# New step orders for the heads of attentions 2 to 4, two masked groups on GpSimd instead of three, and one home for the query operand

## The reference

```python
x = x + _L0_xattn_ref(_layernorm(x), ctx, ctx, fside, mask, ...)   # softmax(QK + mask) * group_prob
x = x + _L1_xattn_ref(_layernorm(x), ctx, ctx, mask, ...)          # where(m == 0, -1e9, scores)
x = x + _L2_xattn_ref(ctx, ctx, _layernorm(x), mask_b, ...)        # one row of key mask
x = x + _L3_xattn_ref(_layernorm(x), ctx, ctx, ...)                # no mask
```

## Time and profile before

| | us |
|---|---|
| runs, timed: median (lowest to highest) | 1549.96 (1547.44 to 1559.05) |
| the profiled execution | 1559.34 |
| its span, first to last instruction | 1558.1 |
| attention 2, second to sixteenth `nmax` | 187.8 |
| attention 3, the same | 169.7 |
| attention 4, the same | 168.6 |

### The profile page before, as it was taken

The page is one execution under the profiler, slowest core; times in us unless marked ns, Lnnn a source line. Parts: engine busy times, 40 slices in busy tenths (PEclk is TensorE's granted clock), DMA queues, the critical chain, the costliest instruction groups (busy, mean ns, idle before and its releaser), DMA issues. The chain is left out here.

```text
span 1558.1 us, 28950 instructions
## 1 busy us (share of the span) xinstructions
PE 1348.7 (87%) x10520; PEld 684.5 (44%) x10594; DVE 1008.2 (65%) x2341; ACT 849.9 (55%) x1302; POOL 518.1 (33%) x700
## 2 busy tenths in 40 slices
PE   6879999799999888599999888599998895999987
PEld 3536567233333356234444455234444582344445
DVE  3524656899999634678886043588885236888832
ACT  1121211799999621189999451167777211777762
POOL 1322011498998810655665330111110002111100
PEclk8989999699999887699999899779999996899999
DMA  6376787111114020111113146112225201112400
GB/s 212 117 223 213 218 252 240 55 43 42 46 36 130 1 68 1 45 52 47 50 49 121 62 120 212 49 37 58 61 62 187 68 0 37 52 52 56 119 2 7
DMA packets 115679, 136.35 MB, mean 88 GB/s; under 512 B 13729, under 2 KB 96841, under 8 KB 113490
## 3 DMA queue, kind: packets, MB, share of 16 engines
q1 hardware_dynamic: 100434, 117.95, 24.4%
q10 hardware_dynamic: 15104, 16.56, 3.7%
HBM read 99.55 MB, written 34.87 MB: 86 GB/s over the span
## 5 line engine op out<-in xcount | busy, mean ns | idle before, releaser
L1150 ACT ACTIVATE prob_a<-ps 128x1024 f32<-128x1024 f32 x464 | 457.5, 1021 | 131.3 <-PE ps L978 90.6
L960 PE MATMUL ps<-kop,qop 52*128 52x512 f16 x1024 | 312.1, 418 | 57.2 <-DVE best_a L1174 19.1
L1174 DVE TENSOR_REDUCE best_a<-ps 128x1 f32<-128x512 f32 (+1 forms) x488 | 315.2, 709 | 52.5 <-PE ps L960 52.2
L978 PE MATMUL ps<-qop,kop 52*128 52x256 f16 x2048 | 246.6, 281 | 6.3 <-ACT prob_a L1150 3.7
L1007 PE MATMUL ps<-prob_a,vop_a 128*32 128x256 f32 x3072 | 211.9, 414 | 7.7 <-ACT qop L1090 3.1
L960 PEld LDWEIGHTS ps<-kop,qop 52*128 52x128 f16 x1024 | 77.0, 95 | 266.8 <-DVE best_a L1174 92.7
L1170 DVE CUSTOM_DVE_ANT_0 dump_a<-ps,neg_q 128x512 bf16<-128x512 f32 (+1 forms) x244 | 163.6, 715 | 43.3 <-PE ps L960 42.0
L1288 POOL TENSOR_TENSOR used_a<-prob_a,gT 128x1024 f32<-128x1024 f32 x64 | 153.0, 2391 | 27.9 <-DVE used_a L1187 17.0
L1266 POOL TENSOR_SCALAR mrest_a<-nmax_a 128x2 f32<-128x2 f32 x64 | 27.8, 434 | 354.2 <-DVE nmax_a L1179 352.9
L978 PEld LDWEIGHTS ps<-qop,kop 52*128 52x128 f16 x2048 | 96.4, 96 | 95.2 <-issue 30.8
L554 ACT ACTIVATE kp<-ps,bk 128x512 f16<-128x512 f32 x64 | 43.8, 687 | 171.1 <-PE ps L486 156.7
(11 more groups left out here) (367 smaller groups left out, 1783.7 us busy)
## 6 DMA issues: line engine op xcount, KB each, us to landing
kop<-kparts SPq DMA_DIRECT2D x384, 64.0 KB, 2.3
vals<-vst SPq DMA_DIRECT2D x16, 1024.0 KB, 4.4
kparts<-kp SPq DMA_DIRECT2D x64, 256.0 KB, 2.3
vraw<-vals SPq DMA_DIRECT2D x64, 256.0 KB, 3.0
e_w<-in_e_w SPq DMA_DIRECT2D x4, 2048.0 KB, 11.8
z_w<-in_z_w SPq DMA_DIRECT2D x24, 256.0 KB, 6.8
ctxT<-in_ctxT SPq DMA_DIRECT2D x8, 512.0 KB, 12.3
raw<-in_mask ACTq DMA_DIRECT2D x16, 256.0 KB, 4.1
```

What stands on the lines that cost most here:

```text
L960: return pe.matmul(out, qop[rows, h, t * P:(t + 1) * P], kop[rows, h % UNROLL, first:first + CHUNK], start=True, stop=True)
L978: ins = pe.matmul(st_bank(n)[:, j * NT:(j + 1) * NT], kop[rows, h % UNROLL, at:at + P], qop[rows, h, :], start=(j % 2 == 0), stop=(not add ...
L1150: act.activation(prob[:, n % NP, :], st_bank(n), ACT.Exp, scale=1.0 / SCORE_UNIT).then_inc(S("exp_done"), 1)
L1174: dve.tensor_reduce(out, bank, AX.X, ALU.max).then_inc(sem, 1)
```

## The change

- New orders. Masked (attention 2) and plain (attentions 3 and 4); value steps now stand one at a time, key steps partly in pairs, and no value step is left for the end of a head as a pair. `SUM_AT` and `TURN_AT` follow. A lower-case `v` (one group) is made possible and not used.
- `SHIELD` is (1, 5): GpSimd masks two groups of a head, TensorE six.
- `qop` is one tile for all four attentions. It is cleared once, by GpSimd in the context stage. The cleared spare rows are copied to DRAM (`clear_rows`), and attentions 2 to 4 clear only the maximum rows (and the mask row) by two DMAs at their start. VectorE's and GpSimd's memsets at those starts are gone; TensorE waits for `rows_cleared` (and `mask_placed`) before its first chunk.
- `NEG` is -(2^27) instead of -(2^100). Queries of blind tokens are multiplied by zero: for attention 1 over the whole of `qop` on GpSimd at the end of the context stage, for attention 2 before the split in high and low parts, which gives three operations in turn (VectorE, ScalarE, VectorE) for two.

```diff
-NEG = -(2.0 ** 100)
+NEG = -(2.0 ** 27)
+FRAME_NEG = -(2.0 ** 100)
...
-MASKED_ORDER = "CCK CCK CCK CVV CCK KCCKF CKCT KCCC VV".replace(" ", "")
-PLAIN_ORDER = "CCKCKCCV CCKCKCV CKCCT KF CKCCKC VV".replace(" ", "")
+MASKED_ORDER = "CCKKCCV CCKKCCCV CKKCF CTKCCV KCCV".replace(" ", "")
+PLAIN_ORDER = "CCKKCCV CKCKCCV KCKCF CCTCKKCV CCV".replace(" ", "")
...
+    def clear_blind(self, dve, S, banks, whole, sighted):
+        for mt in range(CT):
+            dve.wait_ge(S("q_psum"), mt + 1)
+            dve.scalar_tensor_tensor(out=self.half(whole, mt), in0=self.c.ps[:, banks[mt], 0:NT],
+                                     scalar=self.c.bq[:, self.l, mt:mt + 1], in1=sighted[:, :],
+                                     op0=ALU.add, op1=ALU.mult).then_inc(S("q_whole"), 1)
+    def high_of(self, act, S, whole):
+        for mt in range(CT):
+            act.wait_ge(S("q_whole"), mt + 1)
+            act.activation(self.half(self.qp[:, HIGH, :], mt), self.half(whole, mt), ACT.Copy).then_inc(S("q_part0"), 1)
+    def low_of(self, dve, S, whole):
+        for mt in range(CT):
+            dve.wait_ge(S("q_part0"), mt + 1)
+            dve.tensor_tensor(self.half(self.qp[:, LOW, :], mt), self.half(whole, mt), self.half(self.qp[:, HIGH, :], mt),
+                              ALU.subtract).then_inc(S("q_part1"), 1)
...
@@ load_half, load_rest @@
-        eng.wait_ge(S("qop_set"), 1)
-        sp.wait_ge(S("qop_rest_set"), 1)
...
@@ project_context, SP @@
                     if u == 2 * EARLY:
+                        sp.wait_ge(S("qop_set"), 1)
+                        sp.dma_start(c.clear_rows, c.qop[R_MAX:R_LOW, :, :]).then_inc(S("clear_kept"), 16)
                         q.load_half(sp, S, 0)
...
@@ project_context, VectorE and GpSimd @@
-            dve.memset(c.qop[:, 0:UNROLL, :], 0.0).then_inc(S("qop_set"), 1)
-            pool.memset(c.qop[:, UNROLL:H, :], 0.0).then_inc(S("qop_rest_set"), 1)
+            pool.memset(c.qop[:, :, :], 0.0).then_inc(S("qop_set"), 1)
...
                     pool.tensor_scalar(dst, src, -1.0, -NEG, ALU.add, ALU.mult).then_inc(S("mask_made"), 1)
                     pool.wait_ge(S("mask_made"), PIECES * l + i + 1)
+                    if l == 3 and i == PIECES - 1:
+                        pool.wait_ge(S("blind_loaded"), 16)
+                        pool.tensor_scalar(sighted[:, :], blind, -1.0, 1.0, ALU.mult, ALU.add).then_inc(S("sighted"), 1)
+                        pool.wait_ge(S("sighted"), 1)
+                        pool.wait_ge(c.ops.S("q_first"), Q_DONE)
+                        pool.wait_ge(c.ops.S("q_rest"), Q_DONE)
+                        pool.tensor_tensor(c.qop[:, :, :], c.qop[:, :, :], sighted[:, :].unsqueeze(1).to_broadcast((P, H, NT)), ALU.mult)\
+                            .then_inc(S("sighted"), 1)
...
@@ queries @@
         norm_dve(c, dve, S, c.x, c.xn)
-        dve.memset(c.qop[:, 0:UNROLL, :], 0.0).then_inc(S("qop_set"), 1)
-        q.low(dve, S, banks)
         if l == SHIELDED:
             dve.wait_ge(S("masks_summed"), 1)
+            dve.tensor_scalar(sighted[:, :], c.ps[:, 7, 0:NT], (KEYS - 0.5) * NEG, None, ALU.is_gt).then_inc(S("sighted"), 1)
             dve.tensor_scalar(blind[:, :], c.ps[:, 7, 0:NT], (KEYS - 0.5) * NEG, None, ALU.is_le).then_inc(S("blind_found"), 1)
+            dve.wait_ge(S("sighted"), 1)
+            q.clear_blind(dve, S, banks, whole, sighted)
+            q.low_of(dve, S, whole)
+        else:
+            q.low(dve, S, banks)
...
         norm_pool(c, pool, S)
-        pool.memset(c.qop[:, UNROLL:H, :], 0.0).then_inc(S("qop_rest_set"), 1)
...
     def _(sp):
+        for half in range(HALVES):
+            at, rows = half * HROWS + R_MAX, (R_MASK if l == KEYED else R_LOW) - R_MAX
+            sp.dma_start(c.qop[at:at + rows, :, :], c.clear_rows[0:rows, :, :]).then_inc(S("rows_cleared"), 16)
         if l == KEYED:
-            sp.wait_ge(S("qop_set"), 1)
-            sp.wait_ge(S("qop_rest_set"), 1)
...
@@ attend @@
-    SUM_AT, TURN_AT = (1, 1) if weighted else (2, 5) if by_query else (3, 5)
-    SHIELD = (2, 5, 7) if l == SHIELDED else ()
+    SUM_AT, TURN_AT = (1, 1) if weighted else (3, 4) if by_query else (3, 5)
+    SHIELD = (1, 5) if l == SHIELDED else ()
...
-        if l == KEYED:
-            sp.wait_ge(asked.S("mask_placed"), 16 * HALVES)
...
+        if asked is not None:
+            pe.wait_ge(asked.S("rows_cleared"), 16 * HALVES)
+        if l == KEYED:
+            pe.wait_ge(asked.S("mask_placed"), 16 * HALVES)
         for n in range(FIRST):
...
@@ program @@
+        c.qop = sb("qop", [P, H, NT], F16)
```

More of the change, by code:

```diff
@@ L415, in project_context @@
         blind = c.xn[:, 0, :]
+        sighted = sb("sighted", [P, NT], F32)
         best_seen = c.xn[:, 1, 0:QT * 4].rearrange("p (t i) -> p t i", t=QT)
@@ L475, in _ @@
             sp.wait_ge(S("g_loaded"), 16 * NGROUP)
+            sp.wait_ge(S("clear_kept"), 16)
         @block.tensor
@@ L808, in queries @@
     blind = sb("blind", [P, NT], BF16) if l == SHIELDED else None
+    sighted = sb("sighted", [P, NT], F32) if l == SHIELDED else None
+    whole = sb("whole", [P, CT * NT], F32) if l == SHIELDED else None
     stage = Stage(S)
@@ L846, in _ @@
            .then_inc(S("xT_ready"), 1)
-        q.high(act, S, banks)
+        if l == SHIELDED:
+            q.high_of(act, S, whole)
+        else:
+            q.high(act, S, banks)
         q.load_half(act, S, 1)
@@ L1010, in values, with some_values @@
             ins.then_inc(S("pv_psum"), 1)
-        def two_values(first):
-            for n in (first, first + 1):
+        def some_values(groups):
+            for n in groups:
                 if n % NGROUP == 0:
@@ L1068, in _ @@
                     g += 1
-                elif step == "V":
+                elif step in "Vv":
+                    many = 2 if step == "V" else 1
                     if n >= 0:
-                        two_values(n)
-                    n += 2
+                        some_values(range(n, n + many))
+                    n += many
                 elif step == "T" and h + 1 < H:
@@ L1077, in _ @@
         for n in range(NGROUP * H - LAG, NGROUP * H, 2):
-            two_values(n)
+            some_values((n, n + 1))
         fold(H - 1)
@@ L1803, in _ @@
             pool.wait_ge(S("mask"), 1)
-            pool.memset(mask[0:FR, FR:2 * FR], NEG).then_inc(S("mask"), 1)
-            pool.memset(mask[0:FR, P + 3 * FR:P + 4 * FR], NEG).then_inc(S("mask"), 1)
+            pool.memset(mask[0:FR, FR:2 * FR], FRAME_NEG).then_inc(S("mask"), 1)
+            pool.memset(mask[0:FR, P + 3 * FR:P + 4 * FR], FRAME_NEG).then_inc(S("mask"), 1)
             add_bias_pool(c, pool, S, bo)
@@ L2753, in program @@
         c.vals = nc.dram_tensor("vals", (LAYERS, P, KT * D), F32).ap()
+        c.clear_rows = nc.dram_tensor("clear_rows", (R_LOW - R_MAX, H, NT), F16).ap()
         c.ops = Operands(c, ctx)
+        c.qop = sb("qop", [P, H, NT], F16)
         steps = 12 if steps is None else steps
@@ L2763, in program, with load_next @@
                 c.neg_k = sb("neg_k", [P, KT, NT], BF16)
-                with nc.sbuf_tensor("qop0", [P, H, NT], F16) as c.qop:
-                    project_context(c)
-                    with ExitStack() as beside:
-                        for_taylor, for_expert = TaylorWeights(c, beside), FirstExpertWeights(c, beside)
-                        def load_next(sp):
-                            for_taylor.load(sp)
-                            for_expert.load(sp)
-                        cross(c, 0, True, True, load_next)
-                        taylor(c, for_taylor)
-                        first_expert(c, for_expert)
+                project_context(c)
+                with ExitStack() as beside:
+                    for_taylor, for_expert = TaylorWeights(c, beside), FirstExpertWeights(c, beside)
+                    def load_next(sp):
+                        for_taylor.load(sp)
+                        for_expert.load(sp)
+                    cross(c, 0, True, True, load_next)
+                    taylor(c, for_taylor)
+                    first_expert(c, for_expert)
                 cross(c, 1, True, False, for_frames.load)
@@ L2803, in cross @@
         if l > 0:
-            c.qop = ctx.enter_context(c.nc.sbuf_tensor(f"qop{l}", [P, H, NT], F16))
             asked = queries(c, l, ctx)
```

## The result

The changed kernel takes 1497.57 us (median of four runs, 1493.02 to 1500.73) against 1553.18 for the kernel before beside it (1547.44 to 1559.05): ratio 0.964, 95% interval 0.9591 to 0.9688. The forecast was 1516, with a range of 1502 to 1534, so the kernel is faster than the whole range. The sign came out and most of the mechanisms did; the gain was undersized: 56 us by medians, 62.6 by the spans of the two profiled executions (1558.1 and 1495.5), where 34 were forecast.

What follows compares the result with a forecast made beforehand. VectorE, with holes made by TensorE's order, was taken to bound attentions 3 and 4, TensorE attention 2. Terms -9.0 - 9.0 - 8.2 - 4.0 - 6.9 + 2.7 = -34.4, taken as -34 off 1549.96: 1516 us, range 1502 to 1534.

Steps and rivals of the forecast that it cites:

- Part 1: Attentions 3 and 4: the new plain order shrinks VectorE's holes, 10.85 us a head, 9.0 us saved in each attention.
- the walk: Step-by-step costing of a head in attentions 3 and 4: holes of 0.68 us in all, 10.85 us a head.
- (e): Rival, attentions 2 to 4: second key steps of pairs wait for exponentials and block TensorE; 1612 us, chance 0.05.
- (c): Rival, attentions 3 and 4: holes only move and heads stay at 11.54 us; +18, 1534 us, chance 0.11.
- the hole of the pair: Attentions 3 and 4: VectorE's 0.87 us hole after two value steps together, expected to go with the new order.
- The granted clock: Attentions 3 and 4: five of seven heads slowed by TensorE's half clock recover, saving 8.2 us.
- The stretch without value groups: Attentions 3 and 4: the 3.9 us before the clock fell, expected to shorten to about 3.6 us.
- Rival (a): Attentions 3 and 4: slow heads stay as many; +8, 1524 us; chance 0.27 shared with two other rivals.
- Part 2: Attention 2: masked order and two shielded groups, TensorE alone the bound at 13.15 us a head; -4.0 us in all.
- the 1.9 for the shielded group: End of attention 2: the values' wait for GpSimd's masking of the last group disappears, saving 1.9 us.
- Part 3: Starts of attentions 2 to 4: clearing rows by DMA frees the normalisation from GpSimd's memset; -6.9 us.
- Part 4: End of the context stage: GpSimd's new product over qop, 8.5 us, finishes behind VectorE and adds 2.7 us.

Runs made afterwards that it cites:

- x5: Kernel before with the plain order's pair of value steps split, the third value step moved behind the fourteenth chunk: 1589.49 us, ratio 1.0276.
- x6: Kernel before with the turn of the maximum moved one chunk later, behind the fold and the thirteenth chunk: 1526.25 us, ratio 0.9845.
- x9: Kernel before with both plain-order moves, the pair of value steps split and the turn of the maximum later: 1555.77 us, ratio 1.001.
- x1: The kernel before, unchanged, run again for a second trace: 1549.53 us, one execution.
- x3: Kernel before with only the new masked order, two shielded groups and the SUM_AT and TURN_AT places for it: 1545.12 us, ratio 0.9956.
- x10: Kernel before with 30 instead of 16 keep-warm matmuls at the start of attentions 3 and 4: 1544.54 us, one execution.
- x2: Kernel before with the new plain order alone (attentions 3 and 4): 1515.7 us, ratio 0.9773.
- x7: Kernel after with GpSimd's find_seen in attention 2 held until the query's low part is made: 1495.27 us, ratio to before 0.9662.
- x8: Kernel after with GpSimd's product over qop moved ahead of layer 3's mask work in the context stage: 1499.7 us, one execution.
- x11: Kernel after without the mask matmuls of key group 3 in attention 2, so those keys are unmasked: 1498.32 us, one execution.
- x13: Kernel after with find_seen held until the query's third part, and the qop product between layer 2's and layer 3's mask work: 1499.65 us, ratio to before 0.9645.
- x4: Changed kernel with the old orders and three shielded groups, leaving DMA row clearing and the single query operand: 1543.4 us, ratio 0.9934.

## Why the prediction was right in kind and too small in size

The ledger, in us, from the two profiled executions (before, after; "end" is from the last maximum to the last normalised head):

| part | before | after | measured | forecast |
|---|---|---|---|---|
| attentions 3 and 4, 2nd to 16th maximum | 338.5 | 307.3 | -31.2 | -25.7 |
| attention 2, 1st to 16th maximum | 198.5 | 197.9 | -0.6 | -1.1 |
| ends of attentions 2, 3, 4 | 66.5 | 53.6 | -12.9 | -2.9 |
| starts of attentions 2, 3, 4 | 53.4 | 42.4 | -11.0 | -6.9 |
| context stage, attention 1, rest of its layer | 624.9 | 619.8 | -5.0 | +2.7 |
| elsewhere (1.7 of it the output projection of attention 2) | | | -1.9 | 0 |
| sum | | | -62.6 | -33.9 |

**Part 1, the plain order: right.** 10.82 us a head for 10.85 by the walk, 11.55 before: 26 x 0.73 = 19.0 for 18.0. No rival of this part happened: no key step waits for an exponential (e), and the holes did not only move (c). But the hole of the pair was only half of the story: x5 splits the pair, and a wait for the maximum's copies takes the hole's place, larger than it. At the pair's place the copies have been made by then.

**The granted clock: right direction, mis-sized twice.** First, all seven slow heads went, not five (11.6 for 8.2). The stretch without value groups was the wrong measure: it is the same 3.5 us in x6, where nothing falls, and in x9, and the table goes by TensorE's idle time. Second, and larger, I costed the clock from maximum to maximum and gave the ends of the attentions nothing. The ends of x1 and then of the kernel after, attentions 2, 3, 4, in the columns of the earlier trace rows:

```profile
841.50:867.30 25.80, 20.52 (x206) 8.91 (x205) 1.23 (x7) 19.02 (x22) 13.43 (x12) 0.86 0.00 1
1180.10:1201.50 21.40, 17.18 (x191) 8.55 (x190) 1.24 (x7) 13.27 (x18) 1.57 (x6) 0.84 0.01 3
1484.90:1504.30 19.40, 15.39 (x191) 7.61 (x190) 1.26 (x8) 13.29 (x18) 1.57 (x6) 0.91 0.00 1
```
```profile
843.70:864.00 20.30, 19.09 (x208) 7.63 (x207) 1.22 (x7) 15.98 (x20) 8.06 (x10) 1.00 0.01 2
1154.30:1171.00 16.70, 13.49 (x189) 7.16 (x186) 1.25 (x7) 12.72 (x17) 1.57 (x6) 1.00 0.04 13
1434.70:1451.40 16.70, 13.50 (x189) 7.16 (x186) 1.24 (x7) 12.73 (x17) 1.57 (x6) 1.00 0.00 1
```

Granted clocks of 0.86, 0.84 and 0.91 become 1.00. The last head also has its part of the new order's gain: the end of attention 4 takes 18.1 us in x3 with the old order and no half clock, 16.7 with the new one. So in attentions 3 and 4 1.4 a time is order, and the rest, 3.3 and 1.2 us, clock; in attention 2 the old end takes 23.3 us at nearly full clock (x6, x10), 25.8 before and 20.3 after, so 2.5 is clock. This is the step that failed most, 10.0 us in the three ends: "Over 13 heads that is 9.0 us in each attention" left out the last head and what follows it, and the granted clock was counted for heads between maxima alone. In its place the ends gave 7.0 us by the clock and 2.8 by the order.

Part of these 7.0 us is luck of the two executions: of the twelve ends of attentions 3 and 4 in the six profiles with the new plain order (the kernel after, x2, x7, x8, x11, x13) four have 3.4 or 6.8 us at half clock, of the ten with the old one (before, x1, x3, x4, x10) nine. Their mean is 17.3 us for 20.4, a gain of 3.1 an end where the profiled pair has 3.7.

The Trainium skill ("TensorE: Matmul & The Clock Gate", the closing table of rules) asks for long idle gaps between bursts before the clock drops. The traces do not show such gaps: in the head of the earlier trace rows in which the clock fell, TensorE's longest is 0.44 us. Rival (a) did not come about, since the order changed how often the clock falls; less idle time went with fewer falls. What exactly the chip asks for stays open.

**Part 2, attention 2: right for the heads.** 13.2 for 13.15, TensorE without a hole; x11 confirms that TensorE is the bound, with 0.3 us to the next one. That 13.15 came out is in part luck. The 12.70 us busy in the earlier trace rows lack some records (the page counts 10,520 matmuls, that of x1 10,594 for the same code); such a head in x1:

```profile
681.90:695.20 13.30, 13.02 (x129) 5.58 (x128) 10.72 (x36) 12.00 (x14) 7.99 (x10) 1.00 0.18 51
```

TensorE was 13.02 busy and idle for 0.28 where the sum had a need of 12.3 and waits of 1.0, and the change added 0.2 to its busy time, not 0.85. The end was sized 2.9 and gave 5.5 (x3 alone the same): the 1.9 for the shielded group and the Relu of 1.0 were right, as 23.3 to 20.3 us at full clock shows, but the 7.1 us at half clock in that end were not counted.

**Part 3, the starts: the held normalisation right, two terms missed.** In attentions 3 and 4 the gain is 4.6 and 4.3 us, not 2.6. `xn` gives 2.4; the rest is mostly TensorE's clock, since it idles less before the turn of `xn`, and its projection takes 1.99 instead of 3.78 (x10 shows it alone). In attention 2 the forecast of 1.7 met 2.0 by two errors that cancel: the same clock gain, and `low_of` held up by 2.5 us, against the 0.4 I counted. The row was there to read as well as the rule: the Trainium skill ("GPSIMD Engine Reference", Key points) names operations with two SBUF inputs as contending with GpSimd, and here, as in x8, the trace agrees: 3.37 us for two operations of 0.42. I took a low bound where page and the earlier trace rows both pointed to the high one. By the trace the first of the two ended at 629.70 us, 0.29 after the `find_seen` operation beside it, but the second took 1.25 us and ended while the next one ran on to 632.32: a hold, but not always to the other's end.

**Part 4, the context stage's end: right in kind.** The product took 8.00 us and cost 1.5 us behind the last value, forecast 2.7 (2.6 by its own terms, 275.9 less 273.29). But the stage as a whole is less clear. In five profiles with the one query operand (x4, the kernel after, x7, x8, x11) the stage takes 276.7 to 279.9 us; in eight without it, 271.5 to 274.5. Some 4 of these 6 us have arisen by 115 us, long before the product, with half-clock stretches near 60 us, and x13, which has the same code up to there, takes 274.5. What brings those stretches about was not tried.

**Attention 1 and the rest of its layer.** The row of the ledger is +4.4 us up to the first score matmul (274.5 to 278.9) and -9.5 behind it, by no edit of those steps: x1 gives 6.9 of the 9.5 with unchanged code. The forecast of +2.7 was for the stage's end alone. Counted from x1 the change gives 52.8 us of span, near the 55.6 of the medians.

## What to carry to other kernels

A hand-written order of steps is costed to the last instruction of the loop, not from head to head: the end of a stage has its own share of the holes and of the half clock. Where TensorE's clock falls in a tight loop, sum TensorE's idle time in one full-clock iteration, note its longest gap, and try single moves of the step that waits; one letter of an order was worth some 24 us here and another cost 40. Before a step is moved forward, list every wait it carries: a value step moved ahead of the copies it waits for made the loop slower, and an independent GpSimd operation moved beside VectorE work with two SBUF inputs stretched it to nearly the GpSimd operation's own length.

## What the runs showed of the hardware that I had not expected

TensorE's granted clock fell within a loop in which TensorE was busy for over 90% of a head (10.62 of 11.6 us), and stopped falling, past the first heads and up to the last maximum, in the orders with 0.35 to 0.45 us less idle time a head (x2, x6). A VectorE operation beside a GpSimd operation could be held until that one ended (6.93 us for 0.68 in x8), though not every one was: the second `low_of` took 1.25 us for 0.42 beside one of 2.94. Eight projection matmuls took 3.78 or 1.99 us according to whether TensorE had idled 2.98 us before the turn ahead of them.
